# Unread 256-column products in the token layers of a vision tower kernel: ahead of the variances, and between the turns of k and of q

## What is computed

```python
def _linear_attn(x, Wq, Wk, Wv, Wo, bo):        # x: 32 batches, 64 tokens, 64 features; 8 heads of 8
    q = softmax(split(x @ Wq) * scale, axis=-1)  # over the 8 features of a head
    k = softmax(split(x @ Wk) * scale, axis=-2)  # over the tokens
    v = split(x @ Wv)
    context = einsum('bhnd,bhne->bhde', k, v)
    out = einsum('bhnd,bhde->bhne', q, context)
    return merge(out) @ Wo + bo

for i in range(4):
    h = layernorm(x, ln1_g[i], ln1_b[i])
    x = x + _linear_attn(h, Wq[i], Wk[i], Wv[i], Wo[i], bo[i])
    h = layernorm(x, ln2_g[i], ln2_b[i])
    x = x + (gelu(h @ W1[i] + b1[i]) @ W2[i] + b2[i])
```

## Time and profile before

| | us |
|---|---|
| median of 3 runs | 854.49 |
| lowest, highest | 853.65, 860.16 |
| the profiled execution | 850.2 |
| its span, first to last instruction | 848.4 |
| mean granted TensorE clock in it, share of full | 0.855 |
| layers 0 to 3, from the first L1464 to that of the last layernorm (628.17 to 801.57) | 173.4 |

### The profile page before, as it was taken

How to read it: one execution, slowest core, us unless ns; L and a number is a source line. 1 busy time by engine, 2 the same in 40 slices (tenths; PEclk the granted TensorE clock), 3 DMA queues, 4 the chain that set the end, 5 groups by cost and what they waited for, 6 DMA issues and landing times. The chain is left out here.

```text
span 848.4 us, 22240 instructions
## 1 busy us (share of the span) xinstructions
PE 665.2 (78%) x10155; PEld 443.9 (52%) x10155; DVE 561.2 (66%) x858; ACT 361.2 (43%) x485; POOL 49.6 (6%) x88
## 2 busy tenths in 40 slices
PE   3889927776899276678992999777967979797997
PEld 2867613336676132376761334234365858685854
DVE  7859878973688799736887797224047675547453
ACT  0025569100255591002555775331034646364753
POOL 3100000002000000110000000200010202010200
PEclk9989968996899699958996899755987989677999
DMA  8400000023000000320000000400040000000001
GB/s 303 92 2 3 3 0 2 1 87 141 2 2 2 1 1 2 129 98 2 3 2 1 2 2 2 150 20 3 14 179 1 3 1 1 1 1 1 1 1 27
DMA packets 12270, 27.28 MB, mean 32 GB/s; under 512 B 3472, under 2 KB 4368, under 8 KB 12176
## 3 DMA queue, kind: packets, MB, share of 16 engines
q1 hardware_dynamic: 11888, 25.12, 8.8%
q10 hardware_dynamic: 288, 0.73, 0.2%
HBM read 24.80 MB, written 1.05 MB: 30 GB/s over the span
## 5 line engine op out<-in xcount | busy, mean ns | idle before, releaser
L438 ACT ACTIVATE V<-ps,wts 128x1024 f32<-128x1024 f32 x96 | 101.8, 1111 | 252.8 <-PE ps L784 252.8
L612 DVE BATCH_NORM_STATS2 stats<-V 128x6 f32<-128x512 f32 x192 | 117.9, 676 | 15.8 <-ACT V L438 15.6
L488 DVE STREAM_TRANSPOSE A<-V 128x2048 f32<-128x2048 f32 x48 | 107.2, 2273 | 6.7 <-ACT V L389 6.7
L684 PE MATMUL ps<-A,tab 128*128 128x384 f32 x192 | 75.4, 532 | 30.6 <-DVE A L495 30.6
L389 ACT ACTIVATE V<-V,small 128x2048 f32<-128x2048 f32 x48 | 96.6, 2082 | 5.0 <-DVE small L640 5.0
L672 PE MATMUL ps<-A,tab 32*32 32x512 f32 x1536 | 66.6, 654 | 33.8 <-DVE A L488 33.8
L606 DVE STREAM_TRANSPOSE A<-ps 128x2048 f32<-128x2048 f32 x24 | 55.5, 2315 | 36.2 <-PE ps L769 36.1
L684 PEld LDWEIGHTS ps<-A,tab 128*128 128x128 f32 x192 | 36.0, 201 | 80.7 <-DVE A L495 57.4
L784 PEld LDWEIGHTS ps<-tab,A 64*128 64x128 f32 x1024 | 62.5, 195 | 28.0 <-issue 28.0
L495 DVE STREAM_TRANSPOSE A<-ps 128x1024 f32<-128x1024 f32 x48 | 56.7, 1220 | 20.1 <-PE ps L672 20.1
L784 PE MATMUL ps<-tab,A 64*128 64x128 f32 x1024 | 68.8, 286 | 0.0
(11 more groups left out here) (229 smaller groups left out, 919.6 us busy)
## 6 DMA issues: line engine op xcount, KB each, us to landing
A<-in_modes SPq DMA_DIRECT2D x32, 384.0 KB, 6.5
r_ky<-in_modes SPq DMA_DIRECT2D x16, 384.0 KB, 6.4
wl<-in_layers SPq DMA_DIRECT2D x3, 452.0 KB, 5.7
wm<-in_mixture SPq DMA_DIRECT2D x1, 874.5 KB, 8.0
tab<-in_table SPq DMA_DIRECT2D x1, 656.5 KB, 4.9
A<-in_turned SPq DMA_DIRECT2D x1, 512.0 KB, 3.9
V<-in_pixels SPq DMA_DIRECT2D x4, 128.0 KB
tower_out<-A SPq DMA_DIRECT2D x2, 256.0 KB, 2.0
```

The lines of the kernel that those rows point to most:

```text
L438: nc.scalar.activation(Vm[:, 2 * h:2 * h + 2, r, 512 * q:512 * (q + 1)], bank(half_of_u(q, r) + 2 * h, 2).rearrange("p (m n) -> p m n", m= ...
L488: nc.vector.transpose(T[n % 3].rearrange("p (k n) -> p k n", k=16), Vk[:, :, P * n:P * (n + 1)]).then_inc(s_T, 1)
L612: last = nc.vector.bn_stats(stats[:, 16 * q + 4 * r + m, :], Vm[:, m, r, 512 * q:512 * (q + 1)])
L684: last = nc.tensor.matmul(bank(4 + (2 * (u % 2) if l < L - 1 else 0) + pair)[:, 0:MODES * CH], fwd_x[layout][ri], y[:, :, MODES * ri:MODES ...
```

## The change

PE alone gets new instructions. `warm(n)` issues n products of `centre` with the first 256 columns of `cst` into columns 256 to 511 of `bank(0, 1)`. Nothing reads them: v of group 0 lies in columns 0 to 255 of that bank, and the columns behind are next written by the feed-forward product. No semaphore is raised. There are 2 ahead of `variance(l, 0)` in layers 1 to 3, 2 behind each group's k turn, and 3 behind each group's q turn but the last. One wait is added ahead of the k turns: for ScalarE's first copy of v (s_vs), since that copy reads the bank that the added products write. In all 4 x (8 + 9) + 6 = 74 products.

```diff
+            def warm(n):
+
+                for _ in range(n):
+                    nc.tensor.matmul(bank(0, 1, GW), centre, cst[:, 0:GW], start=True, stop=True)
+
             def token_variance(g):
...
             for l in range(DEPTH):
                 w = wl[:, l, :]
+                if l:
+                    warm(2)
                 variance(l, 0)
...
+                pe.wait_ge(s_vs, l * G + 1)
                 for g in range(G):
                     pe.wait_ge(s_ke, l * G + g + 1)
                     pe.wait_ge(s_qs, l * G + g + 1)
                     for t in range(GP):
                         last = nc.tensor.transpose(bank(g, 0, P * t, P), part(ke, g)[:, P * t:P * (t + 1)], ident)
                     last.then_inc(s_ktr, 1)
+                    warm(2)
                 for g in range(G):
                     pe.wait_ge(s_qn, l * G + g + 1)
                     for t in range(GP):
                         last = nc.tensor.transpose(bank(g, 0, GW + P * t, P), part(qs, g)[:, P * t:P * (t + 1)], ident)
                     last.then_inc(s_qtr, 1)
+                    if g < G - 1:
+                        warm(3)
```

## The result

| | before | changed |
|---|---|---|
| median of 4 runs, us | 854.07 | 826.71 |
| lowest to highest | 853.11 to 860.16 | 826.0 to 831.25 |
| the profiled execution | 850.2 | 826.89 |
| its span | 848.4 | 825.1 |
| granted clock over the span | 0.855 | 0.892 |

The changed kernel is faster: ratio 0.9676, 95% interval 0.962 to 0.9733. The prediction said 833, with 825 to 845 as its range. The profiled execution of before is a fifth one, beside the four of the median; that of the changed kernel is one of its four.

The account below looks back on a forecast made before the run. The prediction blamed PE's half clock in the layers, 61.7 us, partly hidden by VectorE's pace. 850.2 less 15.6 (attention) and 4.0 (ahead of variances) gave 830.6; with the unplaced 4.3 us it said 833, range 825 to 845.

Parts of the forecast that it names:

- The mechanism: In the token layers: unread products in PE's waits keep the clock full from k/q/v products to feed-forward, all four layers.
- The sum: Over the profiled execution: 850.2 us less 15.6 in attention and 4.0 ahead of the variances gives 830.6 us.
- Attention, last turn of q to the end of the attention output: At full clock this stretch takes 6.16 us; gains of 1.9, 1.4, 5.3 and 1.5 us in layers 0 to 3.
- Head: Layers 1 to 3, squares to k's first maximum: 1.76 us gained less 0.4 of delay, 4.0 us in three.
- Layer 2's rest at layer 1's length: In layer 2, behind the attention output up to the next layer: 18.73 us becomes 13.22, a gain of 5.5.
- The turns: Between k and q turns: added products cost nothing; q's 1.51 us fits VectorE's 1.69, k's 0.1 us lateness is absorbed.
- The stretch behind the layers: Last layernorm ahead of the mixture: given no term; its variances get no product and may lose the clock as before.
- B: Clock held in attention, not ahead of the variances: 835.8 us, 838 with half of the 4.3 added; chance 0.17.
- C: Layer 2's long half-clock stretch isn't in every run: gain 10.1 us, time 844.4 us; chance 0.18.
- D: Every half-clock microsecond in the layers costs half: 61.7 us cost 30.9, time 820.5 us; chance 0.06.
- E: Clock falls all the same and PE becomes the pace of the turns: 41 us slower, 891 us; chance 0.04.
- The 4.3 us between the profile and the median: Place unknown: 830.6 us if in the token layers, 834.9 if in the stage ahead; 833 was said.

Follow-up runs that it names:

- the thin ones: Changed kernel with each added product of 256 columns replaced by two products of 2 columns: 858.96 us, ratio 1.0166 to the kernel before.

## Why the prediction came out as it did

**The mechanism: shown.** The clock is full in all four layers, and the unread products do it by what they stream: the same PE time filled with products of 2 columns loses it, with transposes of 128 columns keeps it.

**The sum.** In the layers 19.6 us were predicted, and 17.9 measured. The profiled executions differ by 23.3 us: 17.9 in the layers, 1.5 behind them, 3.9 ahead, where nothing was changed. The change itself gave 1.7 us less than the sum said. That the profiled execution still came out at 826.89, under the 830.6 of the sum, is luck: of the stage ahead above all, and of the one behind. On the second chip 18.6 us were measured, a ratio of 0.978, where the forecast's 830.6 / 850.2 is 0.977; that agreement, too, holds the 1.5 us behind the layers. Term by term:

- Attention, last turn of q to the end of the attention output: worked out as 6.16 us, measured 6.52 in all four layers (in layer 1 681.99 to 684.34 + 4.17). The term was 0.36 us too small a layer, 1.4 in four, in two steps: VectorE starts at +1.13, not +0.9, and the last group of the attention output ends 1.16 us behind VectorE's last, not 1.03. That VectorE would be late next, where PE was, is what the rows show.
- Head: its worth was worked out as 7.02 - 5.26 = 1.76 us. The two numbers come from two views; measured as the 7.02 is, from the first variance product to k's first maximum, layer 0 of the kernel before has 5.38, and the changed kernel 5.37. So a held head is worth 1.65 us, 0.1 less, 0.3 in three. The delay was put at 0.4 us and is 0.4 (13.36 to 13.78 us).
- These two make up the 1.7 us by which the layers fell short.
- Layer 2's rest at layer 1's length: right; the two layers are alike to 0.01 us.
- The turns: right. They fit into VectorE's pace, 1.70 us apart, and k's turns come 1.08 us apart as worked out.
- The stretch behind the layers was priced at nothing and gave 1.5 us. It makes up for most of the two terms, by luck: nothing was added there, and whether it takes 45.3 or 46.9 us differs among the kernels here without regard to what stands at the heads.

**The parts don't add up**, which the working had taken for granted by giving each place its own gain. In the layers, the heads alone give 11.2 us, the q turns alone 11.3, the k turns alone 0.1, k and q 17.4, all three 17.9. The long stretch (9.5 us) is counted in both of the first two: either removes it. The k products, worth 0.1 us alone, are worth 6.1 beside those of q: without them the clock falls in or just behind k's turns in three layers, and then some of the q products run at half and hold the turns up. The step that failed is this one: the working gave layer 2's 10.8 us to the attention products alone. These are enough for them, but the heads' two are enough for the long stretch as well. Why one stretch lasts long stays open. In the kernel before the clock falls 16.4 us into layer 1 and 16.3 into layer 2, in the same turns, and comes back after 6.8 us in one and after 27.3 in the other, in both profiles; no run isolates what decides.

**Rivals.** B (held in attention, not at the heads; 835.8 / 850.2 = 0.983) didn't happen in the changed kernel. The kernel without the heads' products shows what it would be: 828.3, a ratio of 0.980, with one head of three falling. C (the long stretch isn't in every run) is refuted for every execution profiled: both profiles of before and that of the k products alone have it in layer 2 (50.7 or 50.8 us), two of them of executions of 844 us. D (each half-clock microsecond costs half, by the Trainium skill's "TensorE: Matmul & The Clock Gate", Terms) would have taken 30.9 us from the layers; 17.9 went, 29% of the 61.7 us, not 50%, since VectorE paced a part of them. E didn't happen in the changed kernel, whose products stay at 0.43 us; its mechanism did with the thin ones.

**The 4.3 us between the profile and the median.** The prediction added half of them. The first set's medians differ by 27.4 us, 8 more than the stages account for. The four executions of before in it have no profile. The untouched stage ahead varied between 620.9 and 628.0 us over 13 profiles, without regard to the kernel, and the medians of before between 844.65 and 854.07 by set. That the rest lies there is likely, but not shown. Some 18 us are what the change is worth in the layers; the first ratio, 0.9676, flatters it.

## What to carry to other kernels

Where PE waits in short steps for another engine and its clock halves, unread products in the waits can keep it full; they must stream columns, since thin products did harm here. Size them so that turn and products fit into the other engine's pace (here 3 x 0.43 + 0.22 under 1.69 us): two products too many cost 0.69 us at each turn. Before giving each half-clock stretch its own price, expect them to hang together, and measure parts alone as well as all but one.

## What was not expected of the hardware

- Transposes hold the clock. The Trainium skill ("TensorE: Matmul & The Clock Gate", Part 4: PE-mode transpose) says that they don't count as work in the same way. This case's trace doesn't agree: streams of eight and twelve fp32 transposes behind the turns kept 1.00 in all layers, 9.8 us on end with nothing else on PE. Here the measurement decides.
- A PE busy for 99.7% of the layers (186.3 of 186.8 us) was granted 0.68 in layer 0 and 0.85 in layer 1, with added products of 2 columns each.
- Within the layers the clock doesn't fall at random: in both profiles of before it falls at the same distances from the first variance product, to 0.1 us, though their times ahead of it differ by 6 us. In all five profiles without products behind k's turns in layer 0, or with thin ones there, the first fall comes 12.3 to 12.5 us behind it. What stands ahead is alike, too: in all 13 profiles with the same code there, the clock comes back to full 1.1 to 1.6 us ahead of the first variance product.
